# Attention scores on two halves of TensorE's rows, and value products in two portions

## The reference

```python
q, k, v = heads(q), heads(k), heads(v)            # qkv = layernorm(x) @ w_qkv.T
attn = jnp.einsum('bhqd,bhkd->bhqk', q, k) / math.sqrt(DK)
mask = jnp.abs(idx[None, :] - idx[:, None]) > WINDOW
attn = jnp.where(mask[None, None], -1000000000.0, attn)
p = jax.nn.softmax(attn, axis=-1)
out = jnp.einsum('bhqk,bhkd->bhqd', p, v)
x = x + jnp.einsum('btc,oc->bto', out, w_proj)
```

## Time and profile before

| | |
|---|---|
| median of 3 runs | 1817.72 us |
| profiled execution | 1817.61 us, span 1815.9 us |
| TensorE busy | 1536.1 us (85%) |
| VectorE busy | 1481.7 us (82%) |
| ScalarE, GpSimd busy | 1268.6 us, 1332.3 us |
| granted TensorE clock, mean | 0.958 |

### The profile page before, as it was taken

The page is one execution under the profiler, slowest core; times in us unless marked ns, Lnnn a source line. Parts: engine busy times, 40 slices in busy tenths (PEclk is TensorE's granted clock), DMA queues, the critical chain, the costliest instruction groups (busy, mean ns, idle before and its releaser), DMA issues.

```text
span 1815.9 us, 37722 instructions
## 1 busy us (share of the span) xinstructions
PE 1536.1 (85%) x11712; PEld 1091.8 (60%) x11712; DVE 1481.7 (82%) x3720; ACT 1268.6 (70%) x1741; POOL 1332.3 (73%) x1579
## 2 busy tenths in 40 slices
PE   3899999999999999768887888878878788887877
PEld 2455555555556666346666766666666666666656
DVE  3668888788888887159899988989889898898988
ACT  1156666666666666558888878888888888788885
POOL 1045555555555555569999999999999999999993
PEclk9689999999999999879999998999999999999999
DMA  5334444443444442100000000000000000000000
GB/s 141 76 81 98 99 97 95 101 96 95 103 103 103 99 99 56 43 29 1 19 18 1 19 18 18 0 18 18 1 18 18 11 8 18 18 0 18 13 6 7
DMA packets 73406, 85.14 MB, mean 47 GB/s; under 512 B 9856, under 2 KB 63616, under 8 KB 68608
## 3 DMA queue, kind: packets, MB, share of 16 engines
q1 hardware_dynamic: 73312, 84.08, 19.7%
HBM read 58.10 MB, written 25.95 MB: 46 GB/s over the span
## 4 chain that ended last, share of the span: by engine, by line
POOL 24%; issue 19%; DVE 7%; ACT 5%; PE 1%; POOLq 0%; DVEq 0%; ACTq 0%; SPq 0%
POOL SUM L751 24%; DVE W L944 4%; ACT E L852 3%; ACT L786 1%; DVE M8Y L888 0%; PE WT L1012 0%; DVE SMALL L888 0%; DVE SMALL L905 0%; ACT GE L785 0%; DVE CT L927 0%; ACT SIM L779 0%; ACT BNT L794 0%; PE MB L979 0%; DVE Z L911 0%; PE E L967 0%
## 5 line engine op out<-in xcount | busy, mean ns | idle before, releaser
L751 POOL TENSOR_TENSOR SUM<-SIM 128x1024 f32<-128x1024 f32 x512 | 959.9, 1912 | 39.8 <-DVE W L944 36.1
L944 DVE SCALAR_TENSOR_TENSOR W<-SUM,SMALL,E 128x1024 f32<-128x1024 f32 x512 | 646.1, 1280 | 86.2 <-ACT E L852 82.1
L852 ACT ACTIVATE E<-SUM,NB 128x1024 f32<-128x1024 f32 x512 | 567.4, 1118 | 136.1 <-DVE W L944 121.6
L1012 PE MATMUL WT<-idf,W 128*128 128x128 f32 x4096 | 554.3, 285 | 104.2 <-DVE CT L927 53.5
L1012 PEld LDWEIGHTS WT<-idf,W 128*128 128x128 f32 x4096 | 476.3, 147 | 274.8 <-DVE W L944 143.0
L264 POOL TENSOR_SCALAR_AFFINE_SELECT PT<-PT 128x128 f32<-128x128 f32 (+1 forms) x1024 | 336.4, 353 | 323.4 <-ACT PT L354 287.2
L409 DVE TENSOR_REDUCE mx<-SX 128x2 f32<-128x512 f32 x256 | 175.4, 685 | 102.7 <-PE SX L492 102.0
L411 DVE TENSOR_REDUCE mx<-SY 128x2 f32<-128x768 f32 x256 | 242.7, 948 | 7.7 <-PE SY L492 7.3
L354 ACT ACTIVATE PT<-TX 128x512 f32<-128x512 f32 x256 | 152.8, 597 | 102.2 <-PE TX L519 100.9
L356 ACT ACTIVATE PT<-TY 128x768 f32<-128x768 f32 x256 | 207.0, 808 | 2.0 <-PE TY L519 0.8
L488 PE MATMUL SY<-K,Q 72*128 72x384 bf16 x512 | 164.0, 343 | 15.6 <-DVE mx L411 14.9
(11 more groups left out here) (111 smaller groups left out, 1671.1 us busy)
## 6 DMA issues: line engine op xcount, KB each, us to landing
K<-k_parts SPq DMA_DIRECT2D x96, 192.0 KB
Q<-q_parts SPq DMA_DIRECT2D x288, 64.0 KB
q_parts<-qp SPq DMA_DIRECT2D x16, 384.0 KB, 2.4
k_parts<-kp SPq DMA_DIRECT2D x16, 384.0 KB, 2.4
xin<-in_x SPq DMA_DIRECT2D x16, 256.0 KB, 3.1
xres<-in_x SPq DMA_DIRECT2D x16, 256.0 KB, 9.0
x<-X SPq DMA_DIRECT2D x16, 256.0 KB, 2.3
x2T<-X2T SPq DMA_DIRECT2D x16, 256.0 KB, 2.1
```

Of the source, the lines that this page charges most:

```text
L751: return eng.tensor_tensor(SUM[(q * FH + h) % RING][:, :].rearrange("p (i j) -> p i j", i=NK), sx, sy, ALU.add)
L852: nc.scalar.activation(E[h % 2][:, :], SUM[(k * FH + h) % RING][:, :], ACT.Exp, bias=NB[q][:, h:h + 1]).then_inc(S["exp_ready"], 1)
L944: nc.vector.scalar_tensor_tensor(out=W[h % WRING][:, :], in0=SUM[(k * FH + h) % RING][:, :], scalar=TOP[q][:, h, TOPK - 1:TOPK], in1=E[h % ...
L1012: o = pe.matmul(WT[:, e, :], W[h % WRING][:, e * P:(e + 1) * P], ident[:, :], is_transpose=True, start=(h == 0 and e % 4 == 0), stop=(h == ...
```

## The change

- The pairs of parts go from nine to six (`TERMS`: the first part of q with three parts of k, the second with two, the third with one): 48 rows. They are loaded twice, at rows 0 to 47 and 64 to 111, and the maxima's three rows come at 112 to 114.
- The scores of the outer tiles and of inner tile 1 are computed on rows 0 to 63 of the array, those of inner tile 2 and all transposed scores on rows 64 to 127. Identity and band are cut in two halves of 64 rows, so `outside` needs two matmuls for each place. `heads` issues scores and transposed scores of a slot in turn.
- A value product is issued in two portions of eight matmuls, in slots sl + 1 and sl + 3.
- VectorE's readers of MB go behind the outer maxima of a slot (`between`), one slot later, and ScalarE's exponentials to the head of its slot; att0 is turned in slot 6 and not in slot 3.
- The loop's unrolled steps change, and the statistics of x2 are taken in the next step.

```diff
-TERMS = 9
-KQ = TERMS * DK
+TERMS = ((0, 3), (1, 2), (2, 1))
+KQ = DK * sum(n for _, n in TERMS)
 SHIFT = 3
+HALF = P // 2
+LOADS = 16 * 2 * sum(1 + n for _, n in TERMS)
...
-VSLOT = ((6, 1), (10, 1), (14, 1), (2, 2))
-ASLOT = (3, 8)
+VSLOT = ((4, 1), (8, 1), (12, 1), (0, 2))
+ASLOT = (6, 8)
...
-        for t in (-1, 0, 1):
+        for t in (-1, 0, 1, 2):
             do(t, t)
-        with eng.Fori(0, 6) as i:
-            do(i * 2 + 2, 2)
+        with eng.Fori(0, 5) as i:
             do(i * 2 + 3, 3)
-        for t in (14, 15, 16, 17):
+            do(i * 2 + 4, 4)
+        for t in (13, 14, 15, 16, 17):
             do(t, t)
 
 
 
-    SHARED = [(1, "mt1", -1, "max_rest", 2, 2), (3, "att0", -2, "att_normed", 2, 1), (4, "xnT", 1, "xnT_ready", 1, 1),
-              (5, "q", 1, "q_rest", 1, 1), (7, "k", 1, "k_rest", 1, 1), (8, "att1", -2, "att_normed", 2, 2),
+    SHARED = [(1, "mt1", -1, "max_rest", 2, 2), (4, "xnT", 1, "xnT_ready", 1, 1), (5, "q", 1, "q_rest", 1, 1),
+              (6, "att0", -2, "att_normed", 2, 1), (7, "k", 1, "k_rest", 1, 1), (8, "att1", -2, "att_normed", 2, 2),
...
-                             k_parts.rearrange("a (d h) n -> (a d) h n", h=H)[:, hs, :]).then_inc(to, 16)
-                for e in range(3):
-                    r = 24 * a + 8 * e
-                    sp.dma_start(Q[b][r:r + 8, hs, :],
-                                 q_parts[a].rearrange("(d h) n -> d h n", h=H)[:, hs, :]).then_inc(to, 16)
+            for r in (0, HALF):
+                for e, n in TERMS:
+                    sp.dma_start(K[b][r:r + DK * n, hs, :],
+                                 k_parts[0:n].rearrange("a (d h) n -> (a d) h n", h=H)[:, hs, :]).then_inc(to, 16)
+                    for a in range(n):
+                        sp.dma_start(Q[b][r + DK * a:r + DK * a + DK, hs, :],
+                                     q_parts[e].rearrange("(d h) n -> d h n", h=H)[:, hs, :]).then_inc(to, 16)
+                    r += DK * n
...
-            sp.dma_start(Q[b][KQ:KQ + 3, hs, :], m_parts[:, hs, :]).then_inc(S["max_rows_loaded"], 16)
+            sp.dma_start(Q[b][HALF + KQ:HALF + KQ + SHIFT, hs, :], m_parts[:, hs, :]).then_inc(S["max_rows_loaded"], 16)
...
+                    nc.scalar.activation(pt[:, 0:512], TX[:, :, :].rearrange("p j n -> p (j n)"), ACT.Exp).then_inc(S["outer_exp"], 1)
+                    act.wait_ge(S["inner_scoresT"], n)
+                    nc.scalar.activation(pt[:, 512:1280].rearrange("p (j n) -> p j n", j=2), TY[:, :, 0:384], ACT.Exp).then_inc(S["inner_exp"], 1)
 
                 if h == 1 and 0 <= c - 1 < SEQS:
-                    shift(t - 1, 2)
+                    shift_part1(t - 1, 2)
+                if h == 2 and 0 <= c - 1 < SEQS:
+                    shift_part2(t - 1, 2)
                 if h == 9 and 0 <= c < SEQS:
-                    shift(t, 1)
+                    shift_part1(t, 1)
+                if h == 10 and 0 <= c < SEQS:
+                    shift_part2(t, 1)
...
+        def x2_stats(t):
+
+            dve.wait_ge(S["x2T_ready"], t + 1)
+            nc.vector.bn_stats(bnst[:, t, :] if isinstance(t, int) else bnst[:, bass.ds(t, 1), :].rearrange("p o n -> p (o n)"), X2T[:, :]).then_inc(S["bn_stats_ready"], 1)
+
+        def between(t, c, h):
+
...
+            if h == 10 and 0 <= c < SEQS:
+                shift_rest(t, 1)
+            if h == 11 and 0 <= c < SEQS:
+                shift_part3(t, 1)
+            for hh, nm, dst, r, sc in ((5, "q", qp, rq, DK ** -0.5), (7, "k", kp, rk, 1.0)):
+                if h == hh + 1 and 0 <= c + 1 < SEQS:
+                    dve.wait_ge(S[nm + "_part1"], t + 2)
...
+                if h == hh + 2 and 0 <= c + 1 < SEQS:
+                    dve.wait_ge(S[nm + "_part2"], t + 2)
...
+            for i, sl in enumerate(ASLOT):
+                if h == sl + 1 and 0 <= c - 2 < SEQS:
+                    n = (t - 2) * 2 + i + 1
+                    dve.wait_ge(S["att_turned"], n)
...
+            if h == 13 and 0 <= c - 2 < SEQS:
+                dve.wait_ge(S["projected"], t - 1)
...
+                nc.vector.tensor_tensor(X1[:, :, :], MB[:, :, :], xres[:, :, :], ALU.add).then_inc(S["x1_ready"], 1)
+            if h == 15 and 0 <= c - 2 < SEQS:
+                dve.wait_ge(S["x1_rstd"], t - 1)
+                norm(X1, tv, trs, X2, S["x2_ready"])
+            if h == 1 and 0 <= c - 3 < SEQS:
+                x2_stats(t - 3)
...
-                    dve.wait_ge(S["inner_scores"], n)
+
+                between(t, c, h)
+
+                if 0 <= c < SEQS:
+                    dve.wait_ge(S["inner_scores"], 2 * n)
                     nc.vector.tensor_reduce(mx[:, h, 1:3], SY[:, :, 0:384], AX.X, ALU.max).then_inc(S["inner_maxima"], 1)
...
+                if h == 14 and 0 <= c - 2 < SEQS:
                     stats(1, t - 2, X1, t6, tv, te, S["x1_stats"], S["x1_means"], S["x1_variance"])
...
+        ROWS_A, ROWS_B = slice(0, HALF), slice(HALF, P)
+
+        def heads(t, c, h):
+
+            scores, scoresT = 0 <= c < SEQS, 0 <= c - 1 < SEQS
+            n, m = t * H + h + 1, (t - 1) * H + h + 1
+            q, k, qT, kT = Q[c % 2], K[c % 2], Q[(c - 1) % 2], K[(c - 1) % 2]
+
+            def tile(out, r, i, k0, k1, clear=True):
+                pe.matmul(out, q[r:r + KQ, h, i * P:(i + 1) * P], k[r:r + KQ, h, k0 * P:k1 * P],
                           start=clear, stop=False, skip_group_check=True)
 
...
+            def outside(out, rows, low, band_):
+                return pe.matmul(out, idb[rows, low, :], bandb[rows, low, band_], start=False, stop=True, skip_group_check=True)
+
+            def tileT(out, j, q0, q1):
+                r = slice(HALF, HALF + KQ + SHIFT)
+                return pe.matmul(out[:, 0:(q1 - q0) * P], kT[r, h, j * P:(j + 1) * P], qT[r, h, q0 * P:q1 * P],
                                  start=True, stop=True, skip_group_check=True)
 
...
+            sx = SX[:, :, :].rearrange("p j n -> p (j n)")
+            if scores:
+                if c > 0 or h > 0:
+                    pe.wait_ge(S["outer_maxima"], n - 1)
+                tile(SX[:, 0, :], 0, 0, 0, 2)
+            if scoresT:
+                if c > 1 or h > 0:
+                    pe.wait_ge(S["outer_exp"], m - 1)
+                tileT(TX[:, 0, :], 0, 0, 2)
+            if scores:
+                tile(SX[:, 1, :], 0, 3, 2, 4, False)
+            if scoresT:
+                tileT(TX[:, 1, :], 3, 2, 4).then_inc(S["outer_scoresT"], 1)
+            if scores:
+                outside(sx[:, P:P + 192], ROWS_A, 0, slice(0, 192))
+            if scoresT:
+                if c > 1 or h > 0:
+                    pe.wait_ge(S["inner_exp"], m - 1)
+                tileT(TY[:, 0, :], 1, 0, 3)
+            if scores:
+                outside(sx[:, P + HALF:3 * P], ROWS_A, 1, slice(HALF, 2 * P)).then_inc(S["outer_scores"], 1)
+            if scoresT:
+                tileT(TY[:, 1, :], 2, 1, 4).then_inc(S["inner_scoresT"], 1)
+            if scores:
+                if c > 0 or h > 0:
+                    pe.wait_ge(S["inner_maxima"], n - 1)
+                tile(SY[:, 0, 0:3 * P], 0, 1, 0, 3)
+                tile(SY[:, 1, 0:3 * P], HALF, 2, 1, 4)
+                for low in range(2):
+                    for i, rows in enumerate((ROWS_A, ROWS_B)):
+                        ends = SY[:, i, :].rearrange("p (a n) -> p a n", n=2 * P)[:, :, 0:P]
+                        o = outside(ends, rows, low, slice(P, 3 * P))
+                        if low:
+                            o.then_inc(S["inner_scores"], 1)
...
-        def values(s, c, g):
...
+            at, q0, q1 = SPAN[j]
+            for e in range(4):
...
+            if j == 3:
+                o.then_inc(S["values_product"], 1)
...
-                if 0 <= c < SEQS:
-                    scores(t, c, h)
+                heads(t, c, h)
...
-                    if h == sl and 0 <= c - ds_ < SEQS:
-                        values(t - ds_, c - ds_, g)
-                if 0 <= c - 1 < SEQS:
-                    scoresT(t, c, h)
+                    if h in (sl + 1, sl + 3) and 0 <= c - ds_ < SEQS:
+                        for j in (0, 1) if h == sl + 1 else (2, 3):
+                            values(t - ds_, c - ds_, g, j)
 
```

More of the change, by code:

```diff
@@ L328, in step @@
                 for g, (sl, ds_) in enumerate(VSLOT):
[L329 removed]
+                    if g % 2 and h == sl + 3 and 0 <= c - ds_ < SEQS:
                         act.wait_ge(S["values_product"], (t - ds_) * 4 + g + 1)
@@ L460, in step @@
                     stats(0, t - 2, X1, t6, tv, te, S["x1_stats"], S["x1_means"], S["x1_variance"])
+                if h == 14 and 0 <= c - 2 < SEQS:
                     stats(1, t - 2, X1, t6, tv, te, S["x1_stats"], S["x1_means"], S["x1_variance"])
-                if h == 14 and 0 <= c - 2 < SEQS:
-                    dve.wait_ge(S["x1_rstd"], t - 1)
-                    norm(X1, tv, trs, X2, S["x2_ready"])
-            if 0 <= c - 2 < SEQS:
-                dve.wait_ge(S["x2T_ready"], t - 1)
```

(57 more changed lines are left out.)

111 lines of the change are left out of this document (42 added, 69 removed).

## The result

The changed kernel takes 1991.4 us (median of 4 runs, 1987.0 to 1995.3) against 1816.9 (1816.0 to 1820.9, 4 runs): ratio 1.0955, 95% interval 1.0925 to 1.0985. The forecast was 1905, its range 1830 to 1975. The direction was right, the size was not: 174 us were lost where 88 were expected.

The account below looks back on a forecast made before the run. TensorE was taken to set the pace at 43.0 us a sequence. Slots with bank waits (47.2) plus a load wait (1.4) gave 48.6; 14 x 5.6 and the ends added 88 to 1817.6: 1905 us, range 1830 to 1975.

Parts of the forecast that it names:

- Halves beside each other: TensorE's scores: both array halves run together, 0.93 us a head instead of 1.45; SX and TX start within some 20 ns.
- Rival 2: TensorE's scores: the halves don't run beside each other, +7 to 8 us a sequence, 2015 us; chance 0.08.
- rivals 3 and 4: Sequence: 3, bank waits cost little, about 1835 us, chance 0.10; 4, loads don't grow, readers early, 1770 us, 0.10.
- Shape changes, 0.13 us each way: TensorE between matmuls of different array shapes: 3.8 us a sequence after, 1.0 before; bounds 0 and 5 us.
- Gain of the halves, 8.3 us: TensorE's scores: 16 heads each 0.52 us shorter, 8.3 us less a sequence.
- the sum is near 44: Slots of a sequence, with free shape changes and early inner scores: near 44 us instead of 47.2.
- Bank waits: TensorE waiting for readers of shared bank MB: stalls of 1 to 2.4 us in six slots; slots sum to 47.2 us.
- The loads: K and Q rows between k store and maxima load: +3.3 us, chain 21.6 us; TensorE waits 1.4 us a sequence.
- The clock, put at full speed in every slot: TensorE's matmul times in the slot sums: taken at the 2.4 GHz level, a lower clock left to rival 1.
- rival 1: TensorE's clock falls to a mean of 0.85: +3.5 us a sequence, 49 us in all, 1955 us; chance 0.17.

Follow-up runs that it names:

- E5: Kernel before with six products instead of nine, contraction kept at 72 rows by zero rows in Q, one copy: 1831.1 us, ratio 1.010.
- E14: E2 without the second copy's loads (half B computes on rows set once; only measures time): 1844.4 us, ratio 1.016.
- E16: E10 with the value products of four heads whole again instead of in two portions (only measures time): 1914.7 us, ratio 1.056.
- E10: Changed kernel without the loads of the second copy, 9 transfers a half instead of 18 (only measures time): 1923.4 us, ratio 1.059.
- E2: Changed kernel's halves and loads, but bank order, readers' places and whole value products as in the kernel before: 1959.7 us, ratio 1.079.
- E4: Kernel before with six products in 48 rows instead of nine in 72, one copy, no halves: 1990.1 us, ratio 1.096.
- E6: E5 with every K and Q load issued twice, the second into rows nothing reads, 18 transfers a half: 1963.1 us, ratio 1.083.
- E8: Changed kernel with 40 unread matmuls of 128 columns filling the wait at a sequence's end: 1988.9 us, ratio 1.098.
- E7: E5 with its one copy in balanced loads, 2 transfers of 48 rows a half: 1829.4 us, ratio 1.008.
- E11: Kernel before with the first chunk of maxima rows loaded ahead of the K and Q rows: 1815.2 us, ratio 0.999.
- E13: E6's bytes in 4 transfers of 48 rows a half, 12 rows on each of 16 engines: 1835.9 us, ratio 1.013.
- E15: E5 with the constant rows set by GpSimd at the start instead of by VectorE: 1813.1 us, ratio 0.999.
- E1: Changed kernel with balanced loads, parts stored in load order and 4 transfers of 48 rows a half: 1943.7 us, ratio 1.070.

## Why the prediction was right in direction and half the size

In us a sequence, each line against the line above:

| change | from | to | |
|---|---|---|---|
| six products, one shape (E5) | 43.06 | 43.05 | 0 |
| halves, old order, one copy (E14) | 43.05 | 45.87 | +2.8 |
| bank order, readers' places and loop of the change (E16) | 45.87 | 50.69 | +4.8 |
| portions of eight (E10) | 50.69 | 51.81 | +1.1 |
| second copy, 18 transfers (after) | 51.81 | 54.51 | +2.7 |

E14's profiled execution is the slowest of its four, 11 us over the median, so its 45.87 may be 0.8 too high. Of the 169 us between the profiled executions of before and after, sequences 2 to 14 lose 146, the start 4, the first two sequences 11, and the last sequence with what follows 8. The sizes hold in this order only: on the old order the second copy costs 6.7 (E14 to E2), on the longer sequence 2.7.

The steps of the prediction:

- **Halves beside each other**: right. Rival 2 is out, and rivals 3 and 4 with it: neither the bank waits nor the loads were small.
- **Shape changes, 0.13 us each way**: right; 0.10 to 0.14 by the starts in E4 and E5.
- **Gain of the halves, 8.3 us**: "With free shape changes and the inner scores starting beside the last transposed tile the sum is near 44" was the nearest I came to pricing the halves. That was in the new order; in the old one, with one copy, E14 measures 45.9, and its losses are half clock in slots 1, 2, 5 and 10 and the waits for code, neither of which is in my sum.
- **Bank waits**: right in place and size at full clock. In the three sequences of the profile (8, 10 and 12) in which the clock is 1.00 throughout slots 3 to 14 these take 35.1 to 35.2 us for my 35.3, and slots 6, 7, 9 and 13 take 2.53, 4.94, 4.10 and 4.25 us for my 2.7, 5.05, 4.25 and 4.3. In the other nine part of the slots runs at 0.50, slot 7 takes up to 6.97 and slot 9 up to 5.29, and slots 3 to 14 take 36.2 to 38.8. Sequence 8, then sequence 9, slots 3 to 14:
```profile
479.00:514.10 35.10, 28.12 (x301) 14.37 (x301) 25.88 (x46) 20.96 (x37) 17.93 (x54) 1.00 0.46 96
532.70:571.20 38.50, 32.35 (x301) 15.46 (x301) 25.24 (x46) 20.89 (x37) 16.77 (x49) 0.87 0.37 77
```
- **The loads, "+3.3 us (bounds 0 and 4.2)"**: mis-sized. From the k store to the maxima load I had 19.2 us, and the mean is 22.7. By rows on the busiest engine the chain is in the mean 15.1 us at 10 (E5), 16.7 at 15 (before), 21.9 at 20 (E6): not the straight 4/3. The growth, 6.0 us, is outside my bounds. I had scaled the load alone and let the maxima rows behind it follow at their old distance; no run separates the two. On a sequence it tells less: the second copy costs 2.7 us (E10 to after) where I had 1.4.
- **The clock, put at full speed in every slot**: the larger failure. I had left it to rival 1 (chance 0.17): "Against it: the stalls are short and scattered." They aren't: norm's wait of 2.5 us and that for the loads lie one behind the other at the end of a sequence, and 0.50 is granted from 299.5, within the first of them, to 313.1, in slot 1 of the next. It costs about 4.2 us a sequence: 1.1 in slot 15's value portion, 1.4 in slots 0 to 2 (E8), 1.7 in slots 3 to 14 (36.8 for 35.1; this one by comparison within the trace alone).
- **Not foreseen: waits for code.** TensorE's matmuls wait for issue between 200 and 600 us in every kernel with halves but E2, and in none without (before, E4 to E7, E11, E13, E15): in sequences two apart, at the edge of the loop over pairs of sequences (3.2 to 3.5 us in E14 and E16), and in slot 1 or 2 (up to 7.0 in E1). Instruction queue 8 brings 32 to 41 packets of 16 KB in these 400 us in the kernels with halves and 1 to 4 in those without. All 42 of the waits over 1 us end 1.4 to 2.5 us after such a packet has landed, while the packets come 10 to 12 us apart in the mean. That is read from the traces; no edit tested it. E2 has the packets too, but no such wait: it stands longer for its maxima rows. The changed kernel itself loses only 4.5 us in the 400 to it, E1 22. Why the loop with halves is fetched anew in every pass, and the one without is not, no run tested; a head has 14 score matmuls there instead of 13.

A sequence of the changed kernel takes 5.9 us more than forecast: 1.6 in slots 0 to 2, 1.5 in slots 3 to 14, 2.8 in slot 15. The half clock's 4.2 and, in slot 15, 1.7 for the longer loads and what code costs make it up; 14 x 5.9 = 83 of the 86 us that the forecast was short. So rival 1, priced at 49 us, came true together with the forecast and not in place of it.

## What to carry to other kernels

Before a contraction is cut to half of the rows, count what runs between in the full shape: at 0.1 us a change, and the lower clock that came with it here, a kernel of short matmuls can lose more than packing saves (E4), and zero rows up to the old shape cost the steady sequence nothing (E5). Choose the rows of a transfer so that all engines share it before counting bytes (E6 and E13: 127 us at equal bytes). Where a change adds a wait to an engine that set the pace, sum the waits that lie next to each other: the clock that falls in them is a term of the forecast, not a rival to it. And where an engine waits for issue, look for instruction packets that land just before it goes on.
